# Batch 1's maxima placed around each step's scores, widest tile first, each behind an unread product of the identity

## The reference

```python
scores = jnp.einsum('bshd,bthd->bhst', q, k) / jnp.sqrt(HEAD_DIM)
scores = jnp.where(causal, scores, -jnp.inf)
probs = jax.nn.softmax(scores, axis=-1)
out = jnp.einsum('bhst,bthd->bshd', probs, v).reshape(B, S, KEY_DIM)
```

## Time and profile before

| | us |
|---|---|
| median of three executions | 652.14 |
| lowest, highest | 641.99, 655.16 |
| the profiled execution | 648.67 |
| its span in the trace | 646.9 |
| PE busy | 467.8 (72%) |
| DVE busy | 341.4 (53%) |
| ACT busy | 234.8 (36%) |
| POOL busy | 179.5 (28%) |

### The profile page before, as it was taken

How to read it: one execution, slowest core, us unless ns; L and a number is a source line. 1 busy time by engine, 2 the same in 40 slices (tenths; PEclk the granted TensorE clock), 3 DMA queues, 4 the chain that set the end, 5 groups by cost and what they waited for, 6 DMA issues and landing times.

```text
span 646.9 us, 8796 instructions
## 1 busy us (share of the span) xinstructions
PE 467.8 (72%) x2581; PEld 296.1 (46%) x2581; DVE 341.4 (53%) x1150; ACT 234.8 (36%) x473; POOL 179.5 (28%) x275
## 2 busy tenths in 40 slices
PE   1876759888786377779376868676669999999410
PEld 1433334433442245326245524443348888886300
DVE  5376684555434672523536136149726766663545
ACT  2222134332554164544235645342033443430215
POOL 5111012211232031321002322111165555504751
PEclk9897765555987598986868877878599999999775
DMA  6000010000000000000000300499035555533332
GB/s 201 16 2 1 8 42 0 2 1 1 0 1 2 0 2 0 17 2 0 1 0 1 99 0 2 152 390 302 7 91 158 163 161 163 163 98 123 105 103 68
DMA packets 29766, 42.82 MB, mean 66 GB/s; under 512 B 3616, under 2 KB 21024, under 8 KB 29728
## 3 DMA queue, kind: packets, MB, share of 16 engines
q1 hardware_dynamic: 25120, 29.74, 13.5%
q0 software_dynamic: 4608, 12.59, 7.4%
HBM read 31.83 MB, written 10.49 MB: 65 GB/s over the span
## 4 chain that ended last, share of the span: by engine, by line
PE 55%; DVE 21%; ACT 8%; issue 7%; POOL 5%; another core or an unknown queue 2%; DMA 2%; SPq 0%; DVEq 0%; ACTq 0%; POOLq 0%
PE PSUM L657 10%; PE PSUM L957 8%; PE PSUM L601 5%; PE PSUM L630 5%; PE PSUM L947 4%; PE PSUM L782 3%; PE PSUM L671 3%; DVE st L1236 2%; POOL QP L583 2%; PE PSUM L938 2%; PE PSUM L607 2%; DVE H L1246 2%; PE PSUM L594 2%; PE PSUM L818 1%
## 5 line engine op out<-in xcount | busy, mean ns | idle before, releaser
L1047 ACT ACTIVATE PR<-PSUM 128x1024 f32<-128x1024 f32 (+1 forms) x96 | 82.1, 880 | 83.1 <-PE PSUM L671 82.8
L536 POOL TENSOR_SCALAR_AFFINE_SELECT PR<-PR 128x256 f32<-128x256 f32 x128 | 52.9, 428 | 177.1 <-ACT PR L1047 176.4
L1317 DVE CUSTOM_DVE_ANT_0 XN<-PSUM,XN 128x128 f32<-128x128 f32 (+3 forms) x128 | 58.1, 489 | 48.4 <-PE PSUM L630 48.1
L573 POOL DMA_INDIRECT QP<-tokens,tok_of x64 | 60.8, 950 | 56.1 <-PE PSUM L938 24.1
L657 PE MATMUL PSUM<-PR,VA 128*32 128x256 f32 (+3 forms) x512 | 60.1, 566 | 12.1 <-DVE XT L1366 9.7
L957 PE MATMUL PSUM<-arena,QP 128*128 x256 | 66.0, 380 | 3.5 <-ACT QP L1196 3.5
L671 PE MATMUL PSUM<-QT,KTr 32*128 32x384 f32 (+7 forms) x256 | 53.0, 450 | 12.8 <-ACT PR L1047 10.2
L630 PE MATMUL PSUM<-KTr,QT 32*128 32x128 f32 (+3 forms) x128 | 43.4, 536 | 14.6 <-DVE mx L1317 14.2
L957 PEld LDWEIGHTS PSUM<-arena,QP 128*128 128x128 f32 x256 | 48.2, 190 | 10.6 <-issue 4.2
L404 POOL TENSOR_TENSOR QP<-QK,QP 128x128 f32<-128x128 f32 (+1 forms) x16 | 9.5, 591 | 148.2 <-ACT QP L397 80.2
L601 PE MATMUL PSUM<-wq_sb,XT 128*128 128x512 f32 x64 | 40.7, 771 | 6.6 <-DVE QK L1298 4.0
(11 more groups left out here) (238 smaller groups left out, 821.9 us busy)
## 6 DMA issues: line engine op xcount, KB each, us to landing
arena<-in_wgu SPq DMA_DIRECT2D x4, 2048.0 KB, 15.7
expert_outputs<-QP SPq DMA_DIRECT2D x64, 128.0 KB
arena<-in_wd SPq DMA_DIRECT2D x2, 2048.0 KB, 16.6
wq_sb<-in_wqkv SPq DMA_DIRECT2D x2, 768.0 KB, 5.4
X<-in_x SPq DMA_DIRECT2D x2, 512.0 KB, 4.6
QP<-in_wsgu SPq DMA_DIRECT2D x1, 1024.0 KB, 5.4
tokens<-XN SPq DMA_DIRECT2D x2, 512.0 KB, 12.8
QP<-tokens,tok_of POOLq DMA_INDIRECT x64
```

Of the source, the lines that this page charges most:

```text
L536: ins = pool.affine_select(diag, diag, [[0, 2], [1, P]], ALU.is_ge, 0.0, base=0, channel_multiplier=-1)
L573: pool.indirect_dma_start(out=XG[:, i % U, :], out_offset=None, in_=h_dram, in_offset=bass.IndirectOffsetOnAxis(ap=tok_of[:, i:i + 1], axis=0)
L1047: did(sc.activation(PR[:, n % PSLOTS, 2 * half:2 * half + 2, 0:WIDTH[chunk]], PSUM[:, 2 * half:2 * half + 2, 0:WIDTH[chunk]], ACT.Exp, sca ...
L1317: did(dv.tensor_tensor_reduce(MSK[m % 2][:, 0:nk], o[:, 0:nk], MASKQ[:, S - nk:S], op0=ALU.add, op1=ALU.max, scale=1.0, scalar=NEG, accum_ ...
```

## The change

`max_plan` writes batch 1's maxima out by step and place. A step has three places: ahead of its scores (0), behind them (1), and behind the weighing (2). Steps 0 to 7 have the 16 maxima of tile 3 (512 wide) in places 0 and 1, steps 8 to 15 those of tile 2, steps 16 to 23 those of tile 1. The heads are chosen so that place 0 and place 1 use the two row groups that the step's scores leave free (scores of rows 0 and 32: heads in rows 64 and 96, and the other way round). Tile 0's (128 wide) stand in place 2 of steps 7 to 22. The turns stand in place 2 of steps 9 (tile 3), 17 (tile 2), 24 (tile 0) and 25 (tile 1).

Ahead of each of the 64 maxima, behind the same wait, PE makes a float32 product of the identity with itself into the same bank, 128 columns wide; the maximum's product writes over it. In the opening, `keep` makes products of the identity with `up_sb`, 256 columns wide, into bank 4: three after each of pairs 28, 29 and 30, eight after pair 31, and three more before the attention. Nobody reads any of these. They add 84 float32 products; the maxima themselves are the same as before, in another order. DVE and ACT follow the same plan, and `ends_tile` tells DVE when a tile is complete.

```diff
--- before.py
+++ after.py
@@ -49,7 +49,24 @@
 TURNS = [(0, 0), (0, 1)] + [(k, b) for b in (0, 1) for k in (1, 2)] + [(3, 0), (3, 1)]
 
 
-TURN_LATER, MAX_STEPS = 5, STEPS + 1
+
+
+def max_plan():
+    order = [2, 0, 6, 4, 10, 8, 14, 12]
+    steps = [[[("max", TB - 1 - step // 8, order[step % 8])], [("max", TB - 1 - step // 8, order[step % 8] + 1)], []]
+             for step in range(STEPS)] + [[[], [], []] for _ in range(LAST_STEP + 1 - STEPS)]
+    for n in range(HEADS0):
+        steps[7 + n][2].append(("max", 0, n))
+    for tile, step in ((3, 9), (2, 17), (0, 24), (1, 25)):
+        steps[step][2].append(("turn", tile))
+    return steps
+
+
+MAX_PLAN = max_plan()
+MAX_STEPS = len(MAX_PLAN)
+MAX_OPS1 = [op for places in MAX_PLAN for ops in places for op in ops]
+UNITS1 = [op[1:] for op in MAX_OPS1 if op[0] == "max"]
+TURNS1 = [op[1] for op in MAX_OPS1 if op[0] == "turn"]
 
 OUT0, LN1, ADD1, NORM2, TURN1, INNER, EXPS, GATED, UP = 0, 6, 6, 11, 13, 17, 19, 22, 27
 LN3, ADD3, NORM4, TURN2, PREP = 28, 30, 33, 39, 41
@@ -64,6 +81,8 @@
 
 LEFT = 4
 NSB = SH * HS // P
+
+KEEP_AT = {28: 3, 29: 3, 30: 3, 31: 8}
 
 
 
@@ -353,15 +372,21 @@
 
             return [(a, 4 * n) for a in (0, 1) for n in range(GROUPS[l] // 4)]
 
-        MUNITS = [(i, n) for i in range(TB) for n in range(HEADS0)]
-        tile_ends = [HEADS0 * (i + 1) - 1 for i in range(TB)]
-        MAX_OPS = [op for m in range(len(MUNITS)) for op in
-                   [("max", m)] + [("turn", i) for i in range(TB - 1) if m == tile_ends[i] + TURN_LATER]] + \
-                  [("turn", TB - 1)]
-
-        def max_ops(step):
-
-            return [(k, op) for k, op in enumerate(MAX_OPS) if k * (MAX_STEPS - 1) // (len(MAX_OPS) - 1) == step]
+        MUNITS = [[(i, n) for i in range(TB) for n in range(HEADS0)], UNITS1]
+        NMAX = len(UNITS1)
+
+        def ends_tile(b, m):
+
+            return all(i != MUNITS[b][m][0] for i, n in MUNITS[b][m + 1:])
+
+        def max_ops(step, place):
+
+            first = sum(len(ops) for places in MAX_PLAN[:step] for ops in places) + sum(len(ops) for ops in MAX_PLAN[step][:place])
+            return list(enumerate(MAX_PLAN[step][place], first))
+
+        def units_to(k):
+
+            return sum(op[0] == "max" for op in MAX_OPS1[:k])
 
         def turn_bank(c, n):
 
@@ -624,15 +649,21 @@
 
             def maxima(b, m, o):
 
-                i, n = MUNITS[m]
+                i, n = MUNITS[b][m]
                 g, row = slot(0, n)
                 nk = (i + 1) * P
                 pe.matmul(o[:, 0:nk], QT[row:row + 32, b, g, i * P:(i + 1) * P], KTr[row:row + 32, b, g, 0:nk],
                           start=True, stop=True).then_inc(s_mps, 1)
 
+            def keep(n, o):
+
+
+                for _ in range(n):
+                    pe.matmul(o[:, 0:D], ident[:, :], up_sb[:, :], start=True, stop=True)
+
             def turn_again(b, i, o):
 
-                pe.wait_ge(s_neg, b * TB + i + 1)
+                pe.wait_ge(s_neg, b * TB + (TURNS1.index(i) if b else i) + 1)
                 for g in range(4):
                     mm = pe.transpose(o[:, g * P:(g + 1) * P], QP0[:, b, i, g * P:(g + 1) * P], ident[:, :])
                 mm.then_inc(s_rqps, 1)
@@ -672,29 +703,36 @@
                                        QT[row:row + SLOT[l], b, g, j * P:S], start=True, stop=True)
                 mm.then_inc(s_sc, 1)
 
-            def attend(l, b, beside, steps):
+            def attend(l, b, beside, steps, around=None):
 
                 for step in range(max(LAST_STEP + 1, steps)):
+                    if around and step < steps:
+                        around(step, 0)
                     if step < STEPS:
                         scores(l, b, step)
+                    if around and step < steps:
+                        around(step, 1)
                     if weighs_at(step):
                         weigh(l, b, *weighs_at(step))
-                    if step < steps:
+                    if around and step < steps:
+                        around(step, 2)
+                    if beside and step < steps:
                         beside(step)
 
-            def max_beside(step):
-
-                for k, (kind, n) in max_ops(step):
+            def max_beside(step, place):
+
+                for k, op in max_ops(step, place):
                     if k >= 2:
-                        before_kind, before_n = MAX_OPS[k - 2]
-                        if before_kind == "max":
-                            pe.wait_ge(s_mrd, len(MUNITS) + before_n + 1)
+                        before = MAX_OPS1[k - 2]
+                        if before[0] == "max":
+                            pe.wait_ge(s_mrd, NMAX + units_to(k - 1))
                         else:
-                            pe.wait_ge(s_rq, TB + before_n + 1)
-                    if kind == "max":
-                        maxima(1, n, bank(6 + k % 2))
+                            pe.wait_ge(s_rq, TB + TURNS1.index(before[1]) + 1)
+                    if op[0] == "max":
+                        pe.matmul(bank(6 + k % 2)[:, 0:P], ident[:, :], ident[:, :], start=True, stop=True)
+                        maxima(1, units_to(k), bank(6 + k % 2))
                     else:
-                        turn_again(1, n, bank(6 + k % 2))
+                        turn_again(1, op[1], bank(6 + k % 2))
 
             def after0(b, step):
 
@@ -862,14 +900,20 @@
                         pe.wait_ge(s_mrd, 2 * (n - 1))
                     for m in (2 * n, 2 * n + 1):
                         maxima(0, m, bank(m % 4))
+                    if n in KEEP_AT:
+                        if n == min(KEEP_AT):
+                            pe.wait_ge(s_qkve, NT)
+                            pe.wait_ge(s_w0, 64)
+                        keep(KEEP_AT[n], bank(4))
             pe.wait_ge(s_tev, 2 * NT)
             pe.wait_ge(s_qkve, NT)
+            keep(3, bank(4))
             pe.wait_ge(s_const, 2)
             pe.wait_ge(s_w0, 64)
             pe.wait_ge(s_ld, 64)
             pe.wait_ge(s_rq, TB)
-            pe.wait_ge(s_mrd, len(MUNITS))
-            attend(0, 0, max_beside, MAX_STEPS)
+            pe.wait_ge(s_mrd, NMAX)
+            attend(0, 0, None, MAX_STEPS, max_beside)
             pe.wait_ge(s_rq, 2 * TB)
             attend(0, 1, lambda step: after0(0, step), AFTER0)
             pe.wait_ge(s_tev, 2 * NT + 2 * TB)
...
@@ -1064,9 +1108,10 @@
                     did(sc.activation(NA, NA, ACT.Exp, scale=-1.0), s_na)
 
             def max_beside(step):
-                for k, (kind, n) in max_ops(step):
-                    if kind == "turn":
-                        store_again(1, n, bank(6 + k % 2))
+                for place in range(3):
+                    for k, op in max_ops(step, place):
+                        if op[0] == "turn":
+                            store_again(1, op[1], bank(6 + k % 2))
 
             def after0(b, step):
                 for r in range(TB // 2):
@@ -1309,14 +1354,14 @@
 
             def maxima(b, m, o):
 
-                i, n = MUNITS[m]
+                i, n = MUNITS[b][m]
                 nk, c = (i + 1) * P, b * TB + i
-                dv.wait_ge(s_mps, b * len(MUNITS) + m + 1)
+                dv.wait_ge(s_mps, b * NMAX + m + 1)
                 if b or m >= 2:
-                    dv.wait_ge(s_mrd, b * len(MUNITS) + m - 1)
+                    dv.wait_ge(s_mrd, b * NMAX + m - 1)
                 did(dv.tensor_tensor_reduce(MSK[m % 2][:, 0:nk], o[:, 0:nk], MASKQ[:, S - nk:S], op0=ALU.add, op1=ALU.max,
                                             scale=1.0, scalar=NEG, accum_out=mx[:, c, n:n + 1]), s_mrd)
-                if n == HEADS0 - 1:
+                if ends_tile(b, m):
 
                     qp = QP0[:, b, i, :].rearrange("p (n c) -> p n c", c=32)
                     settle()
...
```

## The result

The changed kernel takes 674.29 us (median of four, 672.78 to 675.34) against 651.52 for the kernel before (four, 641.99 to 655.16): 1.043 times as long, 95% interval 1.030 to 1.056. Slower, where I had forecast a small gain.

What follows compares the result with a forecast made beforehand. PE, with DVE as partner, was taken to bound layer 0, batch 0's attention at 1.2 GHz. Opening +2.9, bias wait -1.0 and stage -8.3 made -6.4 us, from 652.14 to 645.7 us; range 631 to 662.

Steps and rivals of the forecast that it cites:

- the sum for 2.4 GHz: Attention stage of layer 0, batch 0, at the high clock: trips 40.6, weighing 11.1, turns 2.6, rest 4.3, together 58.6 us.
- I: The new identity product ahead of each maximum in the attention, 64 in all, priced at 0.26 us each.
- W: The weighing products of the attention: 19.51 us before, forecast at 11.1 us at the high clock.
- Trip: Attention: round trip of PE's maximum product, DVE's reading, the way between engines and an identity product; 1.27 us, 32 times.
- rival (d): Attention: PE itself becomes the bound, 58 us with no waiting at all, 650 us for the kernel; chance 0.10.
- rival (a): Attention: clock low all the way, trips of 1.73 us, stage 83.6 us, kernel 670.7 us; chance 0.13.
- The opening: Ahead of the attention: the 20 added products move its start from 92.65 to 95.5 us, +2.9 us.
- The microsecond for DVE's bias: Attention's start: PE no longer waits while DVE adds the bias and computes lambda; -1.0 us.
- Order: Attention: the new order keeps the maxima's number and total width, so the trips' sum does not change.
- (b): Attention: clock falls in steps 0 to 4 and returns with the weighing; +5, 651 us; chance 0.17.
- (c): Attention: weighing hides beside DVE's reading; if 8 of its 11.1 us go, 637.7 us; chance 0.18.

## Why the prediction was wrong

**The step that failed is the clock.** The forecast is the sum for 2.4 GHz, and it rests on "From step 7 there are three I in a step and W's come, and I expect the clock to hold or to come back". The clock held for 9.7 us, fell at step 5 and stayed low until 188.3 us; three identity products a step did not bring it back, and the mean over the stage was 0.56. That the clock decides is shown by the kernel with two identity products: more work, 1.00 throughout, and 22 us less in the stage. That kernel less one product a maximum would need 75.6 - 64 x 0.22 = 61.5 us at 1.00 (an estimate, not run), 3 us more than the 58.6 of the sum. Measured were 97.7. So of the 39 us by which the stage was missed, the clock is about 36.

**The trip was wrong too, and with it the price.** "Trip: 0.41 + 0.49 + 0.11 + 0.26 = 1.27, times 32" lets two maxima share a round trip, one for each bank, but has the identity product in it only once: 8.3 us for 64 products. The one for the other bank was to cost nothing beside it. But PE makes them one after the other, and a full-width product did not overlap with products in 32 rows: each identity product waited for those before it, the 0.43 us of the earlier trace rows that I had put into rival (d), and parted the maxima from the scores. The 0.26 us itself came from two products of L739 in a row, where full-width products follow one another. The second of two costs 0.22 us, so that row was read about rightly; but the first one, after a product in 32 rows, costs 0.42 at the high clock and 0.72 at the low one. So the 64 products cost 64 x 0.42 = 27 us at the high clock, and 64 x 0.72 = 46 at the low one, where the sum had 8.3 and that of rival (a) 16.6 (32 x 0.52). With 512 columns two maxima keep PE for 2 x (0.42 + 0.43) = 1.70 us, longer than the 1.55 of my trip, and nothing waits for DVE any more.

**Where the numbers came near, it was luck.** The estimate of 61.5 us lies close to my 58.6 only because two errors stand against each other: the products cost 19 us more than in the sum, and its 32 waits for DVE, 32 x (0.49 + 0.11) = 19 us, are gone. And rival (a)'s 670.7 us came near the 674.3 measured, but its stage of 83.6 us did not come near 97.7; the time agrees by other parts of the execution.

**A clock that held would have bought little.** The estimated 61.5 us are 5 us under the kernel before, where my sum had 8.3, but above the 59.65 that the new order reaches at the low clock with none of the products: even then they would not have paid.

**The opening.** I forecast 2.9 us more from the first new product to the attention. From pair 28 to the first scores it is 13.4 us (80.10 to 93.50) against 11.0: 2.4 more, and the walk was right in its parts, the eight products ending long after DVE. It did not show, since the pairs themselves came 1.6 us earlier in this execution. The microsecond for DVE's bias came as said.

**Order.** I said that the order leaves the sum of the trips as it is. It gains 7.3 us, and the timeline without identity products shows two maxima and two scores in four row groups starting together. I knew that products of different row groups run over one another and gave the change no credit for putting them side by side. That the whole gain comes from this is argued, not shown.

**Rivals.** (a), to which I gave 0.13, had the clock's course except for its start. (b) needed the clock to return with W, and it did not. (c), W hidden behind waits for DVE, did not come: PE had no idle time left to hide it in. (d), at 0.10, had the mechanism: PE as the bound, by full-width products that wait for those in 32 rows. Its 64 x (0.26 + 0.35) = 39 us were 10 short, by the price of the first product, and its 5 us for scores that no longer overlap stand for nothing, since 64 x (0.42 + 0.35) + 11.1 + 2.6 = 63 us is already more than the estimated 61.5; so its 58 us came out 3 short.

## What to carry to other kernels

A product that is there only to keep TensorE's clock up must be priced where it stands, not in a row of its own kind: between products in a few rows of the array it cost 0.42 us here instead of 0.22, and took away their overlap. Gather such products in one place of a step, on a bank that is overwritten anyway, and put the row-group products side by side; and look at whether the time that the clock gives back is more than what they take. When the clock is at stake, a sum needs both levels, and a run with more of the work is as telling as one with none. And when two banks take turns, count for each engine how often it works in one round trip: here PE made two of each product, and the sum had one.

## What I had not expected of the hardware

- A 128x128 float32 product of the identity kept PE for 0.42 us after a 32-row product and for 0.22 us after one of its own kind (2.4 GHz); at 1.2 GHz for 0.72 us, in 32 rows for 0.45.
- With full-width products once a step, more of them raised the mean granted clock of the stage: 0.54 with none, 0.66 with one product of 128 columns, 0.77 with one of 256, 1.00 with both. Ahead of each maximum it was 0.56 with one and 1.00 with two. Their number alone does not order the kernels: 64 of 128 columns in 97.7 us came with 0.56 (changed kernel), 24 in 59.8 us with 0.66. What else counts stays open.
- PE busy in 85.40 of 85.40 us did not bring the clock up (changed kernel, 102.9 to 188.3).
- The lowest of eleven times of the kernel before was 634.8 us on one chip and 647.4 on another, 2% apart, as much as most effects here.
